# A four-layer mixture kernel: the row mean made once, the second adapter matrix on 128 rows, and stages of the last layers at other steps

## The chip, the cores and the metric

One Trainium2 chip, one core. The metric is device time in microseconds (us): 1599.91 us for the kernel before, median of 3 runs (1598.82 to 1601.06).

## The reference

x has 8 sequences of 256 tokens with 256 features, in float32. Four residual layers follow each other:

```python
x = x + L0(x)   # 2 of 4 experts per sequence (256->1024->256), 3 shared ones, a softmax gate from token 0
x = x + L1(x)   # 8 experts and a shared one, all dense: silu(x @ Wg) * (x @ Wu) @ Wd, weighted per sequence
x = x + L2(x)   # adapter of the sequence's language, then a layer norm
x = x + L3(x)   # y = x @ W[subject].T + b[subject]
```

L2 is the part that the change rewrites most:

```python
h = relu(x @ w1 + b1)                 # 256 -> 64
z = x + h @ w2 + b2                   # 64 -> 256
mean = mean(z); var = mean((z - mean)**2)
L2 = (z - mean) * rsqrt(var + 1e-5) * gamma + beta
```

## The kernel before

The activations lie transposed, features on partitions, in two halves of 128 (`DT` = 2), tokens along the free axis. To keep float32's precision every operand of a product is split into a high and a low part (`fp32r`), and a product is three matmuls: high by high, high by low, low by high (lines 435 to 437). ScalarE copies the high part, VectorE or GpSimd subtracts it for the low part.

L0 and L1 run over blocks of 512 tokens. L1's first eight experts run in 64 stages of `pair_tiles` and `pair_up` (k = 0 to 63), where a scheme of seven products stands for eight. The gate of L0's last block and its mixing into x are not finished when L1 begins: VectorE does them in stages k = 0, 1 and 2. In k = 1 it computes the probabilities (`gate_probs`, lines 1976 to 1978) and mixes the experts' sum ("experts", line 1986) for two sequences behind `gated_tile(k, 2)` and in front of `gated_tile(k, 3)`, and adds x's low part ("lo", line 1988) at the end of the stage. The shared experts follow in k = 2 (line 1990). TensorE's next stage waits for the fourth gated tile.

The ninth (shared) expert of L1, L2 and L3 run together in steps T = 0 to 59 (`last_steps`). A step is one slice of 128 hidden features of one of five jobs: three of 512 tokens, then two of 256 (`LAST_JOBS`). In step T TensorE makes `last_up` of that step (12 products) and `last_down` of step T - 2 (6 products), and then the hooks of the step. From T = 40 on there are hooks alone, but for the last two `last_down`. When job u is complete, VectorE adds it to x (`last_take`, line 2140, in step 8(u+1)), and the unit u of L2 and L3 follows over these tokens, in stages whose steps are written by hand in `WHEN`:

- x2 and xs: x's high and low parts (lines 1359, 2183); for units 1 and 2 the sum of x's two halves (GpSimd, line 1751) and its parts, so that the mean needs two products in place of four.
- up (`l2_up_stage`): x @ w1, 64 output rows. hid: ScalarE makes the relu twice (lines 1383, 1384), VectorE the low part (line 2191), each on 64 rows.
- down (`l2_down_stage`): `mean_part` puts minus the mean of x into both halves of the output in PSUM (lines 810, 814), and three products of w2 with 64 rows each are added to it (lines 834 to 836). w2 and b2 are centred beforehand (lines 2166 to 2175), so that the sum is z less its mean.
- res (line 2202): VectorE adds x and b2. Then the squares (lines 2211, 1760, 1765), gamma (line 1369), the variance (`var_stage`, line 848), eps (line 2218), the power -1/2 (GpSimd, line 1774), a diagonal of it (line 1400), its broadcast by TensorE (`rstd_stage`, line 856), norm and add (lines 2227, 2237), x's new parts, the two halves of L3 (`l3_stage`, lines 872 to 874) and the output with its bias (line 2285).

The last unit (`END`, 4) has a path of its own at the end, in which L3 is applied to parts that are scaled later.

Each engine works its own queue in the order of the program, and within a step in this order: the step's own tile, then the hooks by unit and stage, with those inserted by hand in front or behind. Waits are on semaphores, which count completed instructions of a kind. The banks of `unit_ps` are shared by units 0, 1, 2 and 4: `l2_up_stage` waits for `out_ready`, the output of an earlier unit. SP's queue loads weights; from line 409 on it loads the identity and then, per sequence, w3, w1, w2 and three small vectors (cols: b2, gamma, beta; b1; the bias), into a ring of four buffers `raw`. The eight weights are split in steps 2 to 11 (`center_w2` on VectorE in step b + 2, `late_hi` on ScalarE in b + 3, `late_lo` on GpSimd), and the relu of unit 0 waits for the last of them (line 1377 and after). `b2_stage` (line 785) and `center_b2` (lines 2172 to 2175) centre the bias, in front of all other hooks of step 10.

Of the kernel before, what the change touches and what calls it, by code (L numbers as in the profile page):

```python
# [21 lines left out]
NB = 4  # L22
# [29 lines left out]
STAGES = ["x2", "xs", "up", "hid", "down", "res", "square", "scale", "var", "eps", "diag", "rstd",  # L52
          "norm", "add", "x3", "x3l", "l3a", "outa", "l3b", "outb"]
WHEN = [dict(zip(STAGES, at)) for at in (
# [32 lines left out]
def build(nc, xT_d, sh_d, ex_d, l1_d, types_d, types_row_d, gvec_d, gw1_d, gw2_d, prob_d, sgate_d, w1_d, w2_d, b1_d, cols_d, w3_d, bias_d, ident_d, out_d):  # L87
# [88 lines left out]
    w2 = [place(f"l2_w2_{b}", [A2, 2, D], f32r, over=where_in, skip=2 * K1 * at)  # L176
# [13 lines left out]
    w2s = place("w2_sum", [A2, 1], f32, over="shared_sums", skip=small + 896)  # L190
# [4 lines left out]
    u = place("l2_hidden_r", [A2, 2, BLK], f32r, over="raw", skip=10240)  # L195

    ctx = ExitStack()
    with ctx:
# [40 lines left out]
        small_full = sem("small_full")  # L239
# [10 lines left out]
        hid_relu, sq_first = sem("hid_relu"), sem("sq_first")  # L250
        xs_sum, xs_hi, xs_lo, base_done = sem("x_row_sum"), sem("x_row_hi"), sem("x_row_lo"), sem("base_done")
# [95 lines left out]
        late_small = 3 * B  # L347
# [3 lines left out]
        def _(sp):  # L351
# [58 lines left out]
            for b in range(B):  # L410
                key = ("plain", PLAIN0 + L1_CH * NE1 + b)
# [4 lines left out]
                sp.dma_start(raw[0:A2, s, 640:896], w2_d[langs[b]]).then_inc(raw_full[s], 16)  # L416
                sp.dma_start(cols[:, b], cols_d[langs[b]]).then_inc(small_full, 16)
# [14 lines left out]
        def _(pe):  # L432
# [348 lines left out]
            def b2_stage():  # L781

                pe.wait_ge(small_full, 16 * late_small)
                pe.wait_ge(sum_taken, NB * NJ + 4 * NS)
                pe.matmul(unit_ps[0][:, 1, 0:DT * B], ones[:], cols[:, :, 0:DT], start=True, stop=True).then_inc(b2_sum, 1)

            def l2_up_stage(i):
                b0, nb, t0, c0, n = unit(i)
                pe.wait_ge(w_lo, PLAIN0 + L1_CH * NE1 + b0 + nb)
                if i in (1, 2):  # L790
# [13 lines left out]
            def mean_part(i, m):  # L804
# [3 lines left out]
                if "xs" in WHEN[i]:  # L808
                    for part in range(2):
                        pe.matmul(out, minus_mean[:], xsr[i // 2][:, part, 0:n], start=part == 0, stop=False, skip_group_check=True)  # L810
                    return
# [4 lines left out]

            def l2_down_stage(i):

                b0, nb, t0, c0, n = unit(i)
                if i == 0:  # L820
                    pe.wait_ge(b2_done, 1)
                if "xs" in WHEN[i]:
                    pe.wait_ge(xs_lo, i)
                mean_part(i, 1)
                if i == END:
                    x_part(i, 0)
                pe.wait_ge(hid_relu, i + 1)
                mean_part(i, 0)
                pe.wait_ge(l2_hid, i + 1)
                for b in range(b0, b0 + nb):  # L830
                    c = slice(b % 2 * S, (b % 2 + 1) * S)
                    for m in range(DT):
                        out, k = unit_ps[i][:, m, c], slice(m * P, (m + 1) * P)
                        pe.matmul(out, w2[b][:, 0, k], u[:, 0, c], start=False, stop=False, skip_group_check=True)
                        pe.matmul(out, w2[b][:, 0, k], u[:, 1, c], start=False, stop=False, skip_group_check=True)
                        last = pe.matmul(out, w2[b][:, 1, k], u[:, 0, c], start=False, stop=True, skip_group_check=True)
# [105 lines left out]
            hooks = placed({"up": l2_up_stage, "down": l2_down_stage, "var": var_stage,  # L942
                            "rstd": rstd_stage, "l3a": lambda i: l3_stage(i, 0), "l3b": lambda i: l3_stage(i, 1),
                            "beta": beta_part, "scaled": scaled_part})
            hooks.setdefault(10, []).insert(0, b2_stage)
# [844 lines left out]
        def _(dve):  # L1790
# [278 lines left out]
            def pair_tiles(e, j, s):  # L2069
# [19 lines left out]
                if k == 2:  # L2089
                    mix(0, 0)  # L2090
                    mix(0, 1)
# [276 lines left out]
```

## Time and profile before

| what | value |
|---|---|
| median of 3 runs | 1599.91 us (1598.82 to 1601.06) |
| the profiled execution's own time | 1598.26 us |
| its span | 1596.5 us |
| TensorE busy | 1583.3 us, 99% |
| weight load (beside the matmuls) | 1345.9 us, 84% |
| VectorE busy | 1138.5 us, 71% |
| ScalarE busy | 930.0 us, 58% |
| GpSimd busy | 662.1 us, 41% |
| share of TensorE in the chain that ended last | 93% |
| share of VectorE in that chain | 4% |

The span runs from the first to the last instruction of the profiled execution. In the rows below PE is TensorE, DVE VectorE, ACT ScalarE, POOL GpSimd and SPq the queue of SP. Matmuls are pipelined and their ends are modelled, so that the duration of one is longer than the time that it adds.

### The profile page before, as it was taken

How to read it: one execution, taken by the hardware profiler on the slowest of the kernel's cores; microseconds unless marked ns; L12 is line 12 of the kernel's file. 1: busy time of each engine (PE TensorE's matmuls, PEld its weight loads, DVE VectorE, ACT ScalarE, POOL GpSimd, SP SyncE). 2: the span in 40 equal slices, each digit the busy share in tenths (PEclk: the TensorE clock that was granted, in tenths of full speed). 3: DMA queues.
4: the chain of work that ended last, by engine and by line, in shares of the span. 5: the costliest groups of instructions: out<-in, count | busy, mean ns of one | idle time of the engine just before them, and what ended most of it. 6: DMA issues, size and time to landing. Idle time of an engine off the chain costs nothing.

```text
span 1596.5 us, 22398 instructions
## 1 busy us (share of the span) xinstructions
PE 1583.3 (99%) x7944; PEld 1345.9 (84%) x7944; DVE 1138.5 (71%) x1676; ACT 930.0 (58%) x1680; POOL 662.1 (41%) x576
## 2 busy tenths in 40 slices
PE   9999999999999999999999999999999999999999
PEld 7888888999987888888888888888888888888888
DVE  6755557778889777777776777777777777656556
ACT  5655555665665665565565565565565565554343
POOL 7765544655775431431431431431431431146110
PEclk9999999999999999999999999999999999999999
DMA  4111105455421010010010010010010010021000
GB/s 159 54 54 53 54 27 181 164 185 173 159 84 36 14 41 27 14 40 27 14 40 28 14 40 27 14 40 28 14 41 27 14 40 27 28 58 51 14 14 27
DMA packets 30500, 85.46 MB, mean 54 GB/s; under 512 B 5030, under 2 KB 10022, under 8 KB 30262
## 3 DMA queue, kind: packets, MB, share of 16 engines
q1 hardware_dynamic: 29798, 82.68, 15.1%
q8 instruction: 63, 1.03, 0.3%
q0 software_dynamic: 304, 1.10, 0.2%
q14 instruction: 47, 0.39, 0.1%
q10 hardware_dynamic: 288, 0.26, 0.1%
HBM read 81.93 MB, written 2.10 MB: 53 GB/s over the span
## 4 chain that ended last, share of the span: by engine, by line
PE 93%; DVE 4%; POOL 2%; issue 1%; ACT 1%; DMA 0%; SPq 0%; ACTq 0%; DVEq 0%; POOLq 0%
PE up L666 13%; PE up L668 13%; PE up L667 13%; PE sum L435 12%; PE sum L436 12%; PE sum L437 12%; PE up L435 3%; PE up L436 3%; PE up L437 3%; PE up L443 2%; PE up L444 2%; PE up L445 2%; DVE expert_out L2004 1%; POOL shared_up L1440 1%; DVE hidden L2018 1%
## 5 line engine op out<-in xcount | busy, mean ns | idle before, releaser
L1265 ACT ACTIVATE hidden_hi<-up_tile 128x512 fp32r<-128x512 f32 x256 | 161.2, 630 | 187.7 <-DVE up_tile L2062 163.7
L2057 DVE TENSOR_TENSOR gate_tile<-up,gate_tile 128x512 f32<-128x512 f32 x192 | 129.9, 687 | 141.7 <-PE up L668 141.7
L2067 DVE TENSOR_TENSOR hidden_lo<-up_tile,hidden_hi 128x512 fp32r<-128x512 f32 x256 | 196.7, 788 | 44.7 <-ACT hidden_hi L1265 44.7
L666 PE MATMUL up<-x_sums,gate_up 128*128 128x512 f32 x512 | 199.3, 389 | 0.0
L435 PE MATMUL sum<-hidden_hi,down 128*128 128x512 f32 x512 | 199.3, 389 | 0.0
L437 PE MATMUL sum<-hidden_hi,down 128*128 128x512 f32 x512 | 199.3, 389 | 0.0
L436 PE MATMUL sum<-hidden_lo,down 128*128 128x512 f32 x512 | 199.2, 389 | 0.0
L668 PE MATMUL up<-x_sums,gate_up 128*128 128x512 f32 x512 | 199.2, 389 | 0.0
L667 PE MATMUL up<-x_sums,gate_up 128*128 128x512 f32 x512 | 199.2, 389 | 0.0
L2062 DVE TENSOR_TENSOR up_tile<-up_tile,gate_tile 128x512 f32<-128x512 f32 x192 | 183.8, 983 | 2.3
L1258 ACT ACTIVATE gate_tile<-gate_tile 128x512 f32<-128x512 f32 x192 | 119.7, 632 | 90.4 <-DVE gate_tile L2057 88.3
L1440 POOL TENSOR_TENSOR gate_up<-raw,gate_up 128x384 fp32r<-128x384 f32 x60 | 68.0, 1133 | 204.2 <-ACT gate_up L1209 204.2
L1254 ACT ACTIVATE gate_tile<-up 128x512 f32<-128x512 f32 x192 | 110.6, 594 | 71.2 <-PE up L668 64.8
L666 PE MATMUL up<-x_hi,gate_up 128*128 128x512 f32 x384 | 149.7, 390 | 0.9 <-DVE up_tile L2062 0.9
L667 PE MATMUL up<-x_lo,gate_up 128*128 128x512 f32 x384 | 149.4, 389 | 0.0
L668 PE MATMUL up<-x_hi,gate_up 128*128 128x512 f32 x384 | 149.4, 389 | 0.0
L2057 DVE TENSOR_TENSOR up_tile<-up,up_tile 128x512 f32<-128x512 f32 x192 | 130.0, 687 | 2.6 <-PE up L668 0.7
L1440 POOL TENSOR_TENSOR expert_in<-raw,expert_in 128x512 fp32r<-128x512 f32 x64 | 92.1, 1440 | 89.4 <-ACT expert_in L975 89.3
L1254 ACT ACTIVATE up_tile<-up 128x512 f32<-128x512 f32 x192 | 112.1, 600 | 21.2 <-PE up L668 15.6
L1567 POOL TENSOR_TENSOR weight_sums<-raw 128x256 f32<-128x256 f32 x30 | 28.9, 964 | 204.7 <-PE up L668 204.7
L435 PEld LDWEIGHTS sum<-hidden_hi,down 128*128 128x128 f32 x512 | 96.1, 188 | 20.8 <-DVE hidden_lo L2067 1.2
L666 PEld LDWEIGHTS up<-x_sums,gate_up 128*128 128x128 f32 x512 | 96.1, 188 | 20.3 <-ACT gate_tile L1254 0.4
(323 smaller groups left out, 4031.2 us busy)
## 6 DMA issues: line engine op xcount, KB each, us to landing
raw<-in_experts SPq DMA_DIRECT2D x64, 512.0 KB, 3.2
raw<-in_l SPq DMA_DIRECT2D x51, 512.0 KB, 3.2
raw<-in_shared SPq DMA_DIRECT2D x23, 512.0 KB, 3.3
raw<-in_w SPq DMA_DIRECT2D x8, 256.0 KB, 2.6
x<-in_xT SPq DMA_DIRECT2D x3, 512.0 KB, 9.1
l_stage<-in_l SPq DMA_DIRECT2D x3, 512.0 KB, 4.1
out<-out_stage SPq DMA_DIRECT2D x6, 256.0 KB, 2.6
gate_w<-in_gw POOLq DMA_DIRECT2D x1, 1024.0 KB, 6.1
```

Of the source, the lines that this page charges most:

```text
L435: pe.matmul(out, wh, vh, start=start, stop=False)
L436: pe.matmul(out, wh, vl, start=False, stop=False)
L437: return pe.matmul(out, wl, vh, start=False, stop=stop)
L666: pe.matmul(out, wh, vh, start=first, stop=False, skip_group_check=True)
L667: pe.matmul(out, wh, vl, start=False, stop=False, skip_group_check=True)
L668: return pe.matmul(out, wl, vh, start=False, stop=True, skip_group_check=True)
L1254: A(out, ps, ACT.Copy).then_inc(q_done[m], 1)
L1265: A(hi[:, i], cu[:, i], ACT.Copy).then_inc(hi_done, 1)
L1440: return nc.gpsimd.tensor_tensor(dst, src, hi.bitcast(f32), ALU.subtract)
L2057: V.tensor_tensor(t, ps, t, ALU.add).then_inc(c_done[m], 1)
L2062: V.tensor_tensor(cu[:, i], up, cg[:, RING[i]], ALU.mult).then_inc(gat_done, 1)
L2067: V.tensor_tensor(lo[:, i], cu[:, i], hi[:, i].bitcast(f32), ALU.subtract).then_inc(lo_done, 1)
```

## The change

The mean of x is made once, into the second half of the output (`mean_stage`, at the up stage's step for units 0, 1 and 3, at step 28 for unit 2). VectorE adds it to both halves of x and puts them into y (in `hid_stage`, ahead of the hidden tile's low part), and the residual reads y. w2 is loaded twice, one copy under the other on 128 rows; the high part of the hidden tile stands on rows 0 to 63 and its low part on rows 64 to 127, so that one matmul takes both. The last unit keeps the mean in both halves. Third and fourth unit get other steps, the up stage of units 1 and 2 waits for one output half less, `cols` is loaded ahead of the weights, the bias is centred at the end of step 9's hooks, and the gate's work in stages k = 1 and 2 is ordered anew, with the low part of x added by GpSimd.

```diff
-STAGES = ["x2", "xs", "up", "hid", "down", "res", "square", "scale", "var", "eps", "diag", "rstd",
+STAGES = ["x2", "xs", "up", "mean", "hid", "down", "res", "square", "scale", "var", "eps", "diag", "rstd",
           "norm", "add", "x3", "x3l", "l3a", "outa", "l3b", "outb"]
 WHEN = [dict(zip(STAGES, at)) for at in (
-    (9, 10, 11, 11, 12, 12, 12, 13, 13, 13, 13, 14, 14, 14, 15, 15, 16, 16, 17, 18),
-    (17, 18, 19, 19, 20, 20, 20, 21, 21, 21, 21, 22, 22, 22, 23, 23, 24, 25, 25, 26),
-    (25, 26, 27, 28, 29, 29, 29, 30, 31, 31, 32, 33, 33, 35, 35, 36, 37, 37, 38, 38),
-    (34, 34, 35, 35, 36, 36, 36, 37, 37, 37, 38, 39, 43, 43, 45, 45, 46, 48, 46, 50))]
+    (9, 10, 11, 11, 11, 12, 12, 12, 13, 13, 13, 13, 14, 14, 14, 15, 15, 16, 16, 17, 18),
+    (17, 18, 19, 19, 19, 20, 20, 20, 21, 21, 21, 21, 22, 22, 22, 23, 23, 24, 25, 25, 26),
+    (25, 26, 27, 28, 28, 30, 30, 30, 31, 32, 32, 33, 34, 34, 35, 35, 36, 38, 38, 39, 39),
+    (34, 34, 35, 35, 35, 37, 37, 37, 38, 38, 38, 39, 41, 43, 43, 45, 45, 46, 48, 46, 50))]
...
-    u = place("l2_hidden_r", [A2, 2, BLK], f32r, over="raw", skip=10240)
+    u = place("l2_hidden_r", [2 * A2, BLK], f32r, over="raw", skip=10240)
...
             for b in range(B):
+                sp.dma_start(cols[:, b], cols_d[langs[b]]).then_inc(cols_full, 16)
+            for b in range(B):
...
-                sp.dma_start(raw[0:A2, s, 640:896], w2_d[langs[b]]).then_inc(raw_full[s], 16)
-                sp.dma_start(cols[:, b], cols_d[langs[b]]).then_inc(small_full, 16)
+                sp.dma_start(raw[:, s, 640:896], w2_d[langs[b]]).then_inc(raw_full[s], 16)
...
             def l2_up_stage(i):
...
                 if i in (1, 2):
-                    pe.wait_ge(out_ready, 2 * i)
-                if i == 4:
-                    pe.wait_ge(out_ready, 6)
+                    pe.wait_ge(out_ready, 2 * i - 1)
+                if i == END:
+                    pe.wait_ge(out_ready, 5)
...
+            def mean_stage(i):
+
+                b0, nb, t0, c0, n = unit(i)
+                out = unit_ps[i][:, 1, c0:c0 + n]
                 if i == 0:
                     pe.wait_ge(b2_done, 1)
+                if i in (1, 2):
+                    pe.wait_ge(out_ready, 2 * i)
                 if "xs" in WHEN[i]:
                     pe.wait_ge(xs_lo, i)
-                mean_part(i, 1)
+                    pe.matmul(out, minus_mean[:], xsr[i // 2][:, 0, 0:n], start=True, stop=False)
+                    pe.matmul(out, minus_mean[:], xsr[i // 2][:, 1, 0:n], start=False, stop=True).then_inc(mean_done, 1)
+                    return
+                last = product_of_parts(out, t0, n)
+                last.then_inc(mean_done, 1)
+
+            def product_of_parts(out, t0, n):
+
+                for dt in range(DT):
+                    pe.matmul(out, minus_mean[:], xh[:, dt, t0:t0 + n], start=dt == 0, stop=False)
+                    last = pe.matmul(out, minus_mean[:], xl[:, dt, t0:t0 + n], start=False, stop=dt == DT - 1)
+                return last
+
+            def l2_down_stage(i):
+
+                b0, nb, t0, c0, n = unit(i)
                 if i == END:
+                    pe.wait_ge(out_ready, 6)
+                    mean_part(i, 1)
                     x_part(i, 0)
                 pe.wait_ge(hid_relu, i + 1)
-                mean_part(i, 0)
+                if i == END:
+                    mean_part(i, 0)
+                else:
+                    pe.wait_ge(x_centered, i + 1)
                 pe.wait_ge(l2_hid, i + 1)
...
-                        pe.matmul(out, w2[b][:, 0, k], u[:, 0, c], start=False, stop=False, skip_group_check=True)
-                        pe.matmul(out, w2[b][:, 0, k], u[:, 1, c], start=False, stop=False, skip_group_check=True)
-                        last = pe.matmul(out, w2[b][:, 1, k], u[:, 0, c], start=False, stop=True, skip_group_check=True)
+                        pe.matmul(out, w2[b][:, 0, k], u[:, c], start=i != END, stop=False, skip_group_check=True)
+                        last = pe.matmul(out, w2[b][:, 1, k], u[:, c], start=False, stop=True, skip_group_check=True)
...
-            hooks.setdefault(10, []).insert(0, b2_stage)
+            hooks.setdefault(9, []).insert(0, b2_stage)
...
+                if e == 0:
+                    pool.wait_ge(x_experts, 2)
+                    last_block = slice((NB - 1) * BLK, NB * BLK)
+                    G(x[:, :, last_block], x[:, :, last_block], xl[:, :, last_block].bitcast(f32), ALU.add).then_inc(x_low_added, 1)
                 down_lo(e, 2)
...
             def pair_tiles(e, j, s):
...
                 tile_lo(k, 0)
+                if k == 1:
+                    gate_probs(NB)
+                    mix("experts", 0)
                 if k == 2:
+                    dve.wait_ge(x_low_added, 1)
                     mix(0, 0)
                     mix(0, 1)
...
-                if k == 1:
-                    gate_probs(NB)
-                    mix("experts", 0)
-                    mix("experts", 1)
...
                 tile_lo(k, 1)
                 if k == 1:
-                    mix("lo", 0)
-                    mix("lo", 1)
+                    mix("experts", 1)
...
             def hid_stage(i):
...
+                if i != END:
+                    dve.wait_ge(mean_done, i + 1)
+                    if i:
+                        dve.wait_ge(x3_done, DT * i)
+                    for dt in range(DT):
+                        last = V.tensor_tensor(y[:, dt, c], x[:, dt, t0:t0 + n], unit_ps[i][:, 1, c], ALU.add)
+                    last.then_inc(x_centered, 1)
                 dve.wait_ge(hid_relu, i + 1)
-                V.tensor_tensor(u[:, 1, c], ru[:, c], u[:, 0, c].bitcast(f32), ALU.subtract).then_inc(l2_hid, 1)
+                V.tensor_tensor(u[A2:2 * A2, c], ru[:, c], u[0:A2, c].bitcast(f32), ALU.subtract).then_inc(l2_hid, 1)
...
-            hooks.setdefault(10, []).insert(0, center_b2)
+            hooks.setdefault(9, []).append(center_b2)
...
-        "w2": v["L2_cond_W2"],
+        "w2": np.concatenate([v["L2_cond_W2"], v["L2_cond_W2"]], axis=1),
```

The tiles, copies and sums of w2 go to 128 rows in the same way, and the residual of units 0 to 3 reads y in place of x. GpSimd's new addition stands in front of `down_lo(0, 2)`.

## Rows read from the trace of the kernel before

**Rows 1.** The page, parts 1 (engine, busy us, share, instructions) and 2 (granted clock).

```profile
PE 1583.3 (99%) x7944; PEld 1345.9 (84%) x7944; DVE 1138.5 (71%) x1676; ACT 930.0 (58%) x1680; POOL 662.1 (41%) x576
...
PEclk9999999999999999999999999999999999999999
```

**Rows 2.** TensorE's waits: us in total, times, longest.

```profile
PE sum L435 <- issue: 1.5, 1, 1.5
...
PE up L666 <- DVE up_tile L2062: 0.9, 1, 0.9
...
PE up L814 <- ACT l_hidden_r L1384: 0.8, 1, 0.8
```

**Rows 3.** Timeline of TensorE, unit 0: start, us, engine, line, instruction.

```profile
1463.52 0.28 PE L437 MATMUL sum<-x_hi,l_w 128*64 128x256 f32 x1
1463.63 0.40 PE L435 MATMUL up<-x_hi,last_gate_up 128*128 128x512 f32 x1
1463.86 0.40 PE L436 MATMUL up<-x_lo,last_gate_up 128*128 128x512 f32 x1
...
1469.67 0.39 PE L814 MATMUL sum<-x_lo,minus_mean 128*128 128x512 f32 x1
1469.99 0.38 PE L834 MATMUL sum<-l_hidden_r,l_w 64*128 64x256 f32 x1
1470.22 0.28 PE L835 MATMUL sum<-l_hidden_r,l_w 64*128 64x256 f32 x1
1470.34 0.27 PE L836 MATMUL sum<-l_hidden_r,l_w 64*128 64x256 f32 x1
...
1471.40 0.28 PE L836 MATMUL sum<-l_hidden_r,l_w 64*128 64x256 f32 x1
1471.60 0.50 PE L435 MATMUL up<-x_hi,last_gate_up 128*128 128x512 f32 x1
1471.94 0.40 PE L436 MATMUL up<-x_lo,last_gate_up 128*128 128x512 f32 x1
```

**Rows 4.** Timelines of VectorE and GpSimd, stages k = 1 and 2.

```profile
476.67 1.37 DVE L2057 TENSOR_TENSOR gate_tile<-up,gate_tile 128x512 f32<-128x512 f32 x2 [2.84 <-PE up L668]
...
482.65 1.54 DVE L1986 SCALAR_TENSOR_TENSOR x<-x,gate,x_hi 128x512 f32<-128x512 f32 x2
...
493.83 2.55 POOL L1440 TENSOR_TENSOR down<-raw,down 128x512 fp32r<-128x512 f32 x2 [11.23 <-ACT down L1218]
```

**Rows 5.** Timelines by engine, SP's loads and unit 0.

```profile
1411.11 0.34 SPq L414 DMA_DIRECT2D raw<-in_w  x1
...
1414.13 0.44 SPq L419 DMA_DIRECT2D l_bias<-in_bias  x1
...
1426.83 0.41 DVE L2166 TENSOR_REDUCE w_sum<-raw 64x1 f32<-64x256 f32 x1
...
1464.35 0.22 DVE L2172 TENSOR_SCALAR minus_mean<-ones 128x128 fp32r<-128x128 f32 x1
...
1467.25 0.47 ACT L1383 ACTIVATE l_hidden<-sum,l_b 64x256 f32<-64x256 f32 x1 [0.65 <-POOL l_w L1440]
...
1474.46 1.28 POOL L1765 TENSOR_TENSOR squares<-squares 128x512 f32<-128x512 f32 x1 [0.69 <-DVE squares L2211]
...
1475.84 1.02 PE L848 MATMUL sum<-ones,squares 128*128 128x1 f32 x8
```

**Rows 6.** Timelines by engine: norm of unit 0, then unit 2.

```profile
1482.46 1.28 DVE L2227 TENSOR_TENSOR y<-sum,y 128x512 f32<-128x512 f32 x2
...
1541.21 0.68 DVE L2285 TENSOR_TENSOR out_stage<-sum,l_bias 128x512 f32<-128x512 f32 x1
...
1541.99 0.30 PE L435 MATMUL sum<-x_hi,l_w 128*64 128x256 f32 x1 [1.53 <-issue]
...
1557.95 1.02 POOL L1774 TENSOR_TENSOR rstd<-variance,minus_half 128x4 f32<-128x4 f32 x1 [3.53 <-DVE variance L2218]
...
1559.00 1.28 ACT L1400 ACTIVATE rstd_diag<-ident,rstd 128x128 f32<-128x128 f32 x4 [0.35 <-POOL rstd L1774]
```

More of the change, by code:

```diff
@@ L189, in build @@
     b2s = place("b2_sum", [P, B], f32, over="shared_sums", skip=small + 864)
-    w2s = place("w2_sum", [A2, 1], f32, over="shared_sums", skip=small + 896)
+    w2s = place("w2_sum", [2 * A2, 1], f32, over="shared_sums", skip=small + 896)
     w1r = place("l2_w1", [P, B, 2, DT * A2], f32r, over="gate_w1")
@@ L238, in build @@
         chain = sem("dve_chain")
-        small_full = sem("small_full")
+        small_full, cols_full = sem("small_full"), sem("cols_full")
         x2_done, x2_hi, x2_lo = sem("x2_done"), sem("x2_hi"), sem("x2_lo")
@@ L250, in build @@
         hid_relu, sq_first = sem("hid_relu"), sem("sq_first")
+        x_experts, x_low_added = sem("x_experts"), sem("x_low_added")
+        mean_done, x_centered = sem("mean_done"), sem("x_centered")
         xs_sum, xs_hi, xs_lo, base_done = sem("x_row_sum"), sem("x_row_hi"), sem("x_row_lo"), sem("base_done")
@@ L346, in build @@
         SMALL = 5
-        late_small = 3 * B
+        late_small = 2 * B
         @block.sync
@@ L781, in b2_stage @@
             def b2_stage():
-                pe.wait_ge(small_full, 16 * late_small)
+                pe.wait_ge(cols_full, 16 * B)
                 pe.wait_ge(sum_taken, NB * NJ + 4 * NS)
@@ L807, in mean_part @@
                 out = unit_ps[i][:, m, c0:c0 + n]
[L808 to L811, printed above, removed]
                 for dt in range(DT):
@@ L941, in _ @@
                         pair_up(e, j, s)
-            hooks = placed({"up": l2_up_stage, "down": l2_down_stage, "var": var_stage,
+            hooks = placed({"up": l2_up_stage, "mean": mean_stage, "down": l2_down_stage, "var": var_stage,
                             "rstd": rstd_stage, "l3a": lambda i: l3_stage(i, 0), "l3b": lambda i: l3_stage(i, 1),
                             "beta": beta_part, "scaled": scaled_part})
-            hooks.setdefault(10, []).insert(0, b2_stage)
+            hooks.setdefault(9, []).insert(0, b2_stage)
             def last_step(T, tok, N):
@@ L1383, in hid_hi_stage @@
                     A(ru[:, c], unit_ps[i][0:A2, 0, c], ACT.Relu, bias=b1[:, b:b + 1])
-                    last = A(u[:, 0, c], unit_ps[i][0:A2, 0, c], ACT.Relu, bias=b1[:, b:b + 1])
+                    last = A(u[0:A2, c], unit_ps[i][0:A2, 0, c], ACT.Relu, bias=b1[:, b:b + 1])
                 last.then_inc(hid_relu, 1)
@@ L1991, in mix @@
                                                  ALU.mult, ALU.add)
-                if part != NSH - 1:
+                if part == "experts" and tb == NB:
+                    ins.then_inc(x_experts, 1)
+                elif part != NSH - 1:
                     linked(ins)
@@ L2196, in res_stage @@
                 dve.wait_ge(l2_down, i + 1)
-                if i:
-                    dve.wait_ge(x3_done, DT * min(i, 3))
+                if i == END:
+                    dve.wait_ge(x3_done, DT * 3)
+                else:
+                    dve.wait_ge(x_centered, i + 1)
                 for dt in range(DT):
```

23 lines of the change are left out of this document (13 added, 10 removed).

## The prediction

> **What bounds the kernel now.** Read part 1 of the page first: TensorE is busy for 99% of the span, the next engine for 71% [rows 1], and the granted clock is at its full level in every slice. So a change pays only by what it takes off TensorE's stream or out of its pauses. Then the list of TensorE's waits [rows 2]: they are few. Three of them lie where the change works: 0.9 us behind VectorE's up_tile in the gate's stretch, 1.5 us put down as "issue" and 0.8 us behind the hidden tile. Then the timeline for the pace: the durations (0.39 us) overlap and are no price; what an instruction costs is the distance to the next start, 0.23 us for 512 columns (1463.63, 1463.86) and 0.12 for 256 (1470.22, 1470.34) [rows 3]. One late step is 18 products: 4.08 us with 512 columns (18 x 0.2267), 2.16 with 256.
>
> **The gate (steps of the first expert).** VectorE makes the gate's shares and the mix of both halves (1.54 us) in front of the last gated tile, for which TensorE waits [rows 4]. After the change shares and half a mix stand in front of the tiles of 476.67, where VectorE sat idle for 2.84 us [rows 4]; they need about 1.7 us (0.9 for three small instructions, 0.77 for half of the pair). The other half comes after the last gated tile. The pause goes: 0.9 us and some 0.2 for the restart, 1.1 us. The low part's addition moves to GpSimd, one pass of 1,024 columns; the nearest row is two passes of 512 in 2.55 us [rows 4], so some 2.5. GpSimd was idle for 11.23 us there, until 493.83 [rows 4], and VectorE needs the result only for the next step's mix, some 5 us after. I take nothing; without that cover it would be up to 3 us.
>
> **What leaves TensorE in the five units.** The mean was made in both output halves: units 0 and 3 lose four products, units 1 and 2 two each, 8 x 0.227 + 4 x 0.12 = 2.3 us. The second matrix's three products become two: 16 x 0.12 = 1.9 us. Around these 64-row products lie gaps: 0.32 and 0.23 at the first (1469.67, 1469.99, 1470.22) and, from 1471.40, 0.20 and 0.34 in leaving [rows 3], against 0.23, 0.12, 0.12 and 0.23 by the pace: some 0.4 us a unit, 2.0 in all. Below is nothing, if the gaps belong to the waits that stand at the same places; above is the 0.4. I take 0.4, since a product behind the 64-column stage starts 0.11 after it though it is behind a wait as well (1463.52, 1463.63 [rows 3]). The Trainium skill's page "TensorEngine Tiling (Array Packing)", Key Properties, says that a change of tiling mode drains TensorE, and counts 128x64 as a mode too. By that rule the gain of 2.0 stands, but the 64-column stage should show gaps, and the row shows none; without any drain the sum would be 2.0 smaller.
>
> Were nothing late elsewhere, that would be 6.2 us, with the gate's 1.1 and the waits of the units (1.6, 1.0 and 0.2) 10.1. But the mean's result now goes through VectorE: two additions (1.28 us by [rows 6], the same operands' kinds) stand ahead of the hidden tile's low part, and TensorE waits for both.
>
> **Unit 0.** Centring the bias moves ahead of step 10's tile on VectorE. It is three small instructions, the first 0.22 us [rows 5]; with the waits between them I take 0.5. It was behind the tile; now ScalarE's copy of the tile, the eighth weight's high part and GpSimd's low part come 0.5 later, and the hidden tile, begun at 1467.25, waited for just that (0.65 us behind POOL l_w [rows 5]). Its four copies then end at about 1469.3 and the low part (0.69) near 1470.2. TensorE gets there sooner: 1463.63 + four means 0.93 + a step 4.08 = 1468.6. It pauses 1.6 us, and eight products end at 1471.2, against 1471.60 before [rows 3]: 0.4 gained. VectorE, later by 0.4, makes the squares later too; they ended at 1475.74 (1474.46 + 1.28) and the variance started at 1475.84 [rows 5], so they already decided. They end near 1476.2 while TensorE is there at 1475.3. Net **0.4 lost**. The doubled matrix (128 rows where 64 stood) costs each engine nothing by rows, as durations go by columns; bound above: every one doubled, 0.4 us at each of three engines on this path, 1.5 in all. On SP eight small loads now stand ahead of the first weights; each takes 0.6 us of the queue (1411.11 to 1414.13 is five issues), 5 us together. VectorE's first use of what they delay is at 1426.83 [rows 5], 15.7 after, and each later batch is shorter by 0.6. Nothing; without cover up to 5.
>
> The low part of the hidden tile is written to rows 64 to 127, from rows 0 to 63. The Trainium skill's "VectorE: DVE Perf Modes", "Two Vector instructions with no wait between them", holds such an instruction until the earlier ones have ended, against the overlap of 0.08 us that rows show. By it unit 0 would come another 0.1 to 0.2 later. No row here has such a write; my sum leaves that to the range.
>
> **Unit 1.** Off TensorE go 0.46 (mean), 0.48 (four products) and 0.4 (gaps), 1.3; its hidden tile has a whole step of cover, so no pause there. But VectorE gets to the residual only 0.8 earlier, and the variance hangs on the squares as in unit 0. **0.8 gained**.
>
> **Unit 2.** The 1.5 us "issue" are really the output's second half: VectorE works at it until 1541.89 (1541.21 + 0.68), TensorE starts at 1541.99 [rows 6]. The up stage no longer waits for it, the mean does, one step later: 1.6 gained, plus 0.46, 0.48 and 0.4, is 2.9. Then comes a new wait. The eps now stands on VectorE at step 32, behind the sum taken from step 33's product. From the end of that product 1.3 us for sum and eps, 1.02 for the power and 1.28 for the diagonal [rows 6], with hand-overs 4.0; TensorE needs only one step of 2.16 until it wants it at step 34: a pause of 1.8, where it paused 0.4 to 0.5 before. With the rest **2.0 remain**, bounds 1.0 and 2.9.
>
> **Unit 3.** The 0.8 us pause behind the hidden tile goes, with its restart 1.0; four means, two products and the gaps are 0.48, 0.24 and 0.4: 2.1. Given back are about 0.7 (the low part of x is late, VectorE being busy with unit 2's norm) and 0.9 (the variance, again behind the squares); later pauses of about 0.5 in front of the last unit shrink. **1.0 gained**. **Last unit**: two products 0.24 and the gaps 0.4, **0.6**, for its end is a chain through TensorE.
>
> **The sum** is 1.1 - 0.4 + 0.8 + 2.0 + 1.0 + 0.6 = 5.1 us. The profiled execution took 1598.26 us (span 1596.5 and 1.8 around it), so 1593.2 for it; it lies 1.65 below the median 1599.91, and I forecast the median: **1594.8 us**. About 0.2%, 3.2 us, is what a measurement of this kernel can tell from no change.
>
> **Rivals.**
> *The whole stream is gained* (0.12): VectorE keeps up everywhere, 10.1 us, 1589.8. For it: VectorE is busy only 71%. Against it: in unit 0 the squares and the hidden tile set the time already.
> *Less is gained* (0.20): the 64-row gaps are waits and remain (2.0), and VectorE's hand-overs cost 0.2 more in each of four units: 5.1 - 2.8 = 2.3, 1597.6. For it: at both places with gaps stands a wait.
> *Slower* (0.06): the new pauses at steps 12, 13, 34 and 38 make TensorE's clock fall. Place: from step 34 on, the 1.8 us pause. About 19 us of products follow; at the lower level, 1.2 instead of 2.4 GHz, they take twice that. If half of them run so, it costs 9.5: 1594.8 + 9.5 = 1604. It decides from a third of them on (5.1 us). Against it: the longest pause now, 1.53 us before 1541.99 [rows 6], lies in a slice at the full level, as all do [rows 1].
> *My forecast* (0.62): its own range is 1592 to 1597.
>
> The range, 1590.0 to 1598.6, takes in the forecast's bounds, most of the second case and nearly all of the first, and leaves out the slow one. Faster: 0.55 of the forecast, 0.12 and 0.09, 0.76. Within: 0.18. Slower: 0.06.
>
> **What would show it.** Right: no TensorE wait behind up_tile near 485 and no "issue" near 1540; no 0.2 us gaps around the second matrix; a wait of one to two us behind the hidden tile of unit 0, one before each variance, one behind rstd_diag at step 34. The forecast is wrong if TensorE has none of the new waits (then 1590), if the gaps stay (1597), or if the time changed somewhere outside of 470 to 500 and of the last 140 us.

## The result, and the profile of the kernel after

The changed kernel takes 1593.8 us (median; 1592.89 to 1595.73), the kernel before 1599.45 us in the same sessions: a ratio of 0.9965 with a 95% interval of 0.9952 to 0.9978. That is 5.65 us less, and faster by more than 0.2%. The forecast was 1594.8 us, range 1590.0 to 1598.6.

The page of the kernel after, parts 1 and 2 (its profiled execution took 1593.19 us):

```profile
span 1591.4 us, 22366 instructions
...
PE 1577.5 (99%) x7916; PEld 1342.9 (84%) x7916; DVE 1144.1 (72%) x1682; ACT 929.8 (58%) x1680; POOL 664.8 (42%) x577
...
PEclk9999999999999999999999999999999999999999
```

TensorE has 28 instructions fewer than before [rows 1], twelve means and sixteen products of the second matrix, and is 5.8 us less busy. It still bounds the kernel, at 99%. TensorE's waits in the kernel after (us in total, times, longest):

```profile
PE sum L858 <- DVE l_hidden_r L2226: 1.5, 1, 1.5
PE sum L879 <- ACT rstd_diag L1423: 1.3, 1, 1.3
...
PE sum L871 <- POOL squares L1792: 1.0, 2, 0.7
...
PE up L871 <- DVE squares L2249: 0.4, 1, 0.4
```

All three rows of [rows 2] are gone: "issue", up_tile and ScalarE's hidden tile. In their place stand these four rows, 4.2 us together, at places that the prediction named. One sign of its list is missing: nothing waits in front of unit 2's variance. TensorE's timeline shows where each stands: unit 0's second matrix, unit 0's variance, unit 2's rstd, unit 3's variance.

```profile
1468.04 0.39 PE L440 MATMUL sum<-hidden_hi,last_down 128*128 128x512 f32 x1
1469.88 0.36 PE L858 MATMUL sum<-l_hidden_r,l_w 128*128 128x256 f32 x1 [1.46 <-DVE l_hidden_r L2226]
1470.08 0.28 PE L859 MATMUL sum<-l_hidden_r,l_w 128*128 128x256 f32 x1
...
1475.85 1.05 PE L871 MATMUL sum<-ones,squares 128*128 128x1 f32 x8 [0.67 <-POOL squares L1792]
...
1559.87 1.13 PE L879 MATMUL sum<-rstd_diag,ones 128*128 128x512 f32 x2 [1.29 <-ACT rstd_diag L1423]
...
1573.32 1.02 PE L871 MATMUL up<-ones,squares 128*128 128x1 f32 x8 [0.43 <-DVE squares L2249]
```

What a single profiled execution says of a few tenths depends on where one measures. The distance between two products of TensorE that both kernels have is what to compare; in the late steps it repeats from run to run to within 0.1 us, where whole times scatter by 2. "First matrix" is the first 64-column product of a unit, rstd is L856 before and L879 after:

| stretch on TensorE | before | after | difference | forecast |
|---|---|---|---|---|
| gate: last product with expert_out (456.70, 457.48) to the first with gate_up after the pairs of k = 1 to 3 (511.05, 510.74) | 54.35 | 53.26 | -1.09 | -1.1 |
| first late product to unit 0's first matrix | 50.56 | 50.57 | 0 | 0 |
| to unit 0's rstd | 18.67 | 19.12 | +0.45 | +0.4 |
| to unit 1's rstd | 41.58 | 40.84 | -0.74 | -0.8 |
| to unit 3's first matrix | 43.09 | 41.31 | -1.78 | -2.0 |
| to the last unit's first matrix | 20.00 | 18.05 | -1.95 | -1.0 |
| to the end of the last product | 8.12 | 7.48 | -0.64 | -0.6 |

The sum is -5.75, against -5.65 by the medians. Between the gate's stretch and the late steps the kernels differ by 0.1 us in 900. Ahead of the gate's stretch the profiled execution of the kernel after is 0.78 us the longer one (457.48 against 456.70), though the program is the same there; the last section shows a fall of the clock in that part. The forecast's 0.7 us for the low part of x in front of unit 3 stands in its unit 3, but in the table that wait ends the row above, "to unit 3's first matrix". From unit 0's first matrix to the end it is 131.46 us before and 126.80 after; below this is called **the tail**, and the experiments are read by it.

The gate's stretch on VectorE and GpSimd, after:

```profile
474.55 0.15 DVE L2003 TENSOR_REDUCE gate_sum<-gate_exp 128x2 f32<-128x8 f32 x1
...
475.85 1.47 DVE L2013 SCALAR_TENSOR_TENSOR x<-x,gate,x_hi 128x512 f32<-128x512 f32 x1
...
485.13 2.78 POOL L1731 TENSOR_TENSOR x<-x,x_lo 128x1024 f32<-128x1024 f32 x1 [1.29 <-DVE x L2013]
493.52 2.56 POOL L1463 TENSOR_TENSOR down<-raw,down 128x512 fp32r<-128x512 f32 x2 [5.60 <-ACT down L1241]
```

Shares and half a mix now run from 474.55 on, in the time in which VectorE was idle [rows 4]; they take 2.8 us and not 1.7, and still fit. The three small instructions take 1.3 us, as they did before (1.28, from 481.37 to 482.65), where the prediction had 0.9; the half mix takes 1.47 beside GpSimd's weights, where it had 0.77. GpSimd's pass takes 2.78 us (2.5 forecast), and GpSimd is idle behind it for another 5.60. Beside that pass one low part of VectorE, of 512 columns, took 2.29 us in place of 0.68 (at 486.18); TensorE waited for nothing there.

### The profile page after: what moved, and what is told of

Read it like the earlier page. It is cut to its first block, busy times and chain, and to the rows that moved or that the text cites. A ratio compares the mean times of both kernels' runs of the same rounds, so it can differ in the third digit from the quotient of the medians.

```text
span 1591.4 us, 22366 instructions
## 1 busy us (share of the span) xinstructions
PE 1577.5 (99%) x7916; PEld 1342.9 (84%) x7916; DVE 1144.1 (72%) x1682; ACT 929.8 (58%) x1680; POOL 664.8 (42%) x577
## 4 chain that ended last, share of the span: by engine, by line
PE 92%; DVE 5%; POOL 2%; ACT 1%; issue 1%; DMA 0%; SPq 0%; ACTq 0%; POOLq 0%; DVEq 0%
PE up L669 13%; PE up L670 13%; PE up L671 13%; PE sum L438 12%; PE sum L439 12%; PE sum L440 12%; PE up L438 3%; PE up L439 3%; PE up L440 3%; PE up L446 2%; PE up L447 2%; PE up L448 2%; DVE expert_out L2033 1%; POOL shared_up L1463 1%; DVE hidden L2047 1%
```

## The experiments

Each edit is to the changed kernel, unless it says otherwise. The kernel before measured 1599.1 to 1599.7 us beside them.

### The gate's order of before

```
 k == 1, in front of the tiles:   - gate_probs(NB); mix("experts", 0)
 in front of the last gated tile: + gate_probs(NB); mix("experts", 0); mix("experts", 1)
 behind it:  - mix("experts", 1)   + mix("lo", 0); mix("lo", 1)
 GpSimd:     - x = x + x_lo
```

> The changed kernel with the gate's order of before: shares and both halves of the experts' mix in front of the last gated tile of step 2, the low part added by VectorE. Theory (the gate is worth 1.1 us): the time is 1.1 us above the changed kernel's 1593.8, so 1594.9, and TensorE shows again a wait of 0.9 us behind up_tile; the stretch from the start of the gate's steps to the first product of the next step group takes 57.0 us as before, not 56.0. Rival (the 1.1 us less in that stretch is not the order of VectorE's work but the scatter of one profiled execution): 1593.8, and no wait behind up_tile.

Measured: 1594.96 us, ratio 0.9971 (0.9960 to 0.9982). The gate's stretch took 54.36 us, against 53.26 after and 54.35 before, and the pause was back. The expectation's 57.0 and 56.0 are the same stretch begun some 2.7 us earlier; they differ by 1.0. TensorE's timeline of this kernel:

```profile
487.43 0.50 PE L669 MATMUL up<-x_hi,gate_up 128*128 128x512 f32 x1 [0.85 <-DVE up_tile L2085]
```

The tail stayed at 126.72. So the gate's part is worth 1.1 us, and by itself.

### 64 rows in place of 128

```
- pe.matmul(out, w2[b][:, 0, k], u[:, c], ...)
+ pe.matmul(out, w2[b][0:A2, 0, k], u[0:A2, c], ...)      (the same for part 1)
```

> The changed kernel with its two products of the second matrix reading rows 0 to 63 alone of weight and hidden tile (same count, same waits, same columns; it leaves out the product of the hidden tile's low part). Theory of the forecast (passing from 128 rows to 64 and back costs TensorE 0.2 us each way): gaps of 0.3 where the first of these products starts and of 0.2 more behind the last, in each of five units; 2.0 us if all of it stands on the path, so 1595.8, and at least 1594.6 if the variance waits of three units absorb theirs. Rival (the gaps of before were the waits that stood at the same places): products 0.12 us apart as with 128 rows, 1593.8.

Measured: 1594.3 us, ratio 0.9970 (0.9958 to 0.9982); the tail is 127.46, 0.66 more. TensorE's timeline of this kernel in unit 1, where TensorE is held up by nothing:

```profile
1511.22 0.39 PE L440 MATMUL sum<-hidden_hi,last_down 128*128 128x512 f32 x1
1511.54 0.38 PE L858 MATMUL sum<-l_hidden_r,l_w 64*128 64x256 f32 x1
1511.76 0.28 PE L859 MATMUL sum<-l_hidden_r,l_w 64*128 64x256 f32 x1
1511.88 0.28 PE L858 MATMUL sum<-l_hidden_r,l_w 64*128 64x256 f32 x1
...
1512.47 0.28 PE L859 MATMUL sum<-l_hidden_r,l_w 64*128 64x256 f32 x1
1512.67 0.50 PE L438 MATMUL up<-x_hi,last_gate_up 128*128 128x512 f32 x1
```

With no pause at either end the gaps are back: 0.32 and 0.22 on entering, 0.20 in leaving, where the pace gives 0.23, 0.12 and 0.12. With the one behind (0.34 for 0.23) that is 0.38 us a unit. The same place of the kernel with 128 rows, with the same semaphore waits in the program, has 0.12 from one product to the next and 0.23 behind the 512 columns. So the gaps belong to the rows and not to the waits: the rival of hand-overs falls. But the tail grew by 0.66 and not by 1.9: in units 0, 1 and 3 the wait in front of the variance shrank by the same amount (0.67 to 0.47, 0.33 and 0.43 to none listed), and only unit 2 (0.3) and the last unit (0.4) pay.

### The doubled matrix alone, on the kernel before

```
- w2[b] [A2, 2, D], u [A2, 2, BLK];  three products: hi x hi, hi x lo, lo x hi
+ w2[b] [2 * A2, 2, D], u [2 * A2, BLK];  two products of 128 rows
```

> The kernel before with the doubled second matrix alone: two products of 128 rows in place of three of 64, the low part of the hidden tile written to rows 64 to 127; steps, means, bias and gate as before. Theory: 1.9 us of products and up to 2.0 us of gaps go, in units 0 to 3 a part of it is given back in front of the variance (0.1 to 0.4 a unit, since the residual starts earlier by the same and VectorE is free for it), so 3.0 to 3.9 us below the kernel before (1599.45), 1595.5 to 1596.5; the doubled work of three engines costs nothing. Rival one (gaps are waits): 1.9 us, 1597.6. Rival two (the write to the other rows, or the doubled weight work, costs on the path): under 1.5 us gained.

Measured: 1597.11 us, ratio 0.9982 (0.9973 to 0.9991); tail 128.80, 2.66 less than before. That is under both ends of the theory (3.0 to 3.9) and above rival one. By the table's stretches it gains 0.17 in unit 0 and 0.60 to 0.64 in each of the others. The products and gaps of units 1 and 2 add up to 0.86 (0.48 + 0.38), and 0.2 of it is given back; unit 3 and the last unit keep their 0.62 (0.24 + 0.38) whole. The weight work of 128 rows delayed nothing: the hidden tile's first copy starts 5.0 us behind unit 0's first product in both kernels. The write to rows 64 to 127 took 0.69 us, as did the one to the other half, but VectorE's next instruction started 0.72 us behind it and not 0.61.

### The relaxed wait of the first matrix alone, on the kernel before

```
 up:   - pe.wait_ge(out_ready, 2 * i)      + pe.wait_ge(out_ready, 2 * i - 1)
 down: + pe.wait_ge(out_ready, 2 * i)      (in front of the means)
```

> The kernel before with one change: the first products of units 1 and 2 wait for the first half of the output before them, and the mean for the second half. Theory (the 1.5 us put down as issue at unit 2 is the wait for the output's second half): that pause goes and nothing takes its place, since the mean stands 0.23 us x 12 and more behind; 1.5 us less, 1597.9, and no issue in TensorE's waits. Rival (it is a pause of TensorE's own queue, or the mean now waits in its place): no gain, or the pause stands at the mean, 1599.45.

Measured: 1598.11 us, ratio 0.9993 (0.9984 to 1.0002), which is 1.6 below the 1599.73 beside it but can't be told from no change by its interval. The tail can tell: 129.73, 1.73 less, all of it in front of unit 2, and TensorE's list has no "issue" any more. The pause of [rows 6] was the wait for the output's second half.

### Both of these parts, on the kernel before

The last two diffs together.

> The kernel before with the doubled second matrix and the relaxed wait of the first matrix's products together: means still made in both output halves, steps and gate as before. Theory (the two parts add up, and the mean made once with its moved steps is worth only the rest): stretch 131.5 - 2.7 - 1.7 = 127.1 against 126.8 of the changed kernel, so the mean made once gave 0.3 us net of the 2.3 us of products that it takes off; 1595.0. Rival (the mean made once gave its 2.3): the two parts don't add up, stretch 129, 1597.

Measured: 1595.39 us, ratio 0.9975 (0.9965 to 0.9985); tail 127.10, as expected to the tenth. So the two parts add up, and the rest of the change, the mean made once with the steps and the bias moved for it, takes the tail from 127.10 to 126.80 only. By the table's stretches this rest loses 0.60 us to unit 0's rstd and 0.59 between unit 1's rstd and unit 3's first matrix, and gains 0.09 in unit 1 and 1.35 in unit 3, where the pause behind the hidden tile and those in front of the last unit go. So of the 2.3 us of products that it removes, 2.0 were given back, net of the pauses that it ends.

### The steps of before for units 2 and 3

```
 unit 2: - down 30, var 32, diag 33, rstd 34     + down 29, var 31, diag 32, rstd 33
 unit 3: - down 37, var 38, diag 39, rstd 41     + down 36, var 37, diag 38, rstd 39
 (and the stages beside them, such as eps, scale and unit 2's L3, one step earlier)
```

> The changed kernel with the steps of before for units 2 and 3 (second matrix at 29 and 36, variance at 31 and 37, rstd at 33 and 39), the mean at 28 and 35. Theory (with the additions ahead of it the hidden tile needs a second step of cover): TensorE waits some 0.3 us behind unit 2's hidden tile and 1.5 us behind unit 3's, against 0.9 us saved at rstd_diag: 0.9 us more, 1594.7. Rival (the moved steps were what gave the gain): the 1.5 to 2 us of units 2 and 3 go, 1597. Rival two (they did nothing): 1593.8.

Measured: 1594.05 us, ratio 0.9970 (0.9959 to 0.9980); tail 127.86, 1.06 more. TensorE's waits in this kernel:

```profile
PE sum L858 <- DVE l_hidden_r L2226: 2.0, 2, 1.5
PE up L858 <- DVE l_hidden_r L2226: 1.3, 1, 1.3
...
PE sum L879 <- ACT rstd_diag L1423: 0.4, 1, 0.4
```

0.5 at unit 2's hidden tile (2.0 less unit 0's 1.5), 1.3 at unit 3's, 0.4 at the diagonal (from 1.3, so 0.9 saved): the theory's 0.3, 1.5 and 0.9. The moved steps are what the additions on VectorE need, and worth 1.1 us with them.

### The bias centred two steps earlier

```
- hooks.setdefault(9, []).insert(0, b2_stage)     + hooks.setdefault(7, []).insert(0, b2_stage)
- hooks.setdefault(9, []).append(center_b2)       + hooks.setdefault(7, []).append(center_b2)
```

> The changed kernel with the centring of the bias two steps earlier, on TensorE and on VectorE. Theory (what the change moved ahead of step 10's tile, 0.42 us, stands on the chain to unit 0's hidden tile): TensorE's wait behind that tile falls from 1.46 to 1.0 us, 0.4 us less in all, 1593.4. Rival (ScalarE or GpSimd has slack there): the wait stays at 1.4 to 1.5.

Measured: 1592.67 us, ratio 0.9961 (0.9946 to 0.9976); tail 126.54, 0.26 less; the wait fell from 1.46 to 1.27. The direction is the theory's, the size half. TensorE's own product for the bias costs 0.24 us with its gaps (1453.22 to 1453.91 in the kernel after, where the pace gives 0.45). It stood right behind the sum that VectorE takes into x, and now stands two steps ahead of it; so that sum, step 9's tile and the low part of x came 0.24 us later, measured from unit 0's first matrix, and of 0.42 us 0.18 were left.

### The eighth weight at step 9

```
 VectorE: center_w2(7)  - at the end of step 9     + at the head of step 9's extra work
 ScalarE: late_hi(7)    - at the head of step 10   + at the end of step 9's extra work
```

> The changed kernel with the eighth weight made ready earlier: centred at the head of step 9's extra work on VectorE (idle there for 0.86 us), its high part at the end of ScalarE's step 9 instead of step 10. Theory (unit 0's hidden tile is late because ScalarE waits for GpSimd's low part of this weight, and nothing else): the wait of 1.46 us behind the hidden tile goes, unit 0 ends 1.0 to 1.5 us earlier, 1592.3 to 1592.8. Rival one (VectorE's two additions are what is late): the wait stays above 1.0, since they start behind step 10's low part at 1467.75 in any case. Rival two (the variance waits in its place): TensorE gets there earlier and waits 1.5 to 2 us behind the squares instead of 0.7; gain under 0.5.

Measured: 1592.62 us, ratio 0.9960 (0.9946 to 0.9973); tail 126.28, 0.52 less. The wait behind the hidden tile halved, to 0.70, which is neither the theory (gone) nor rival one (above 1.0), and the variance did not take over: it stayed at 0.67. VectorE's timeline of this kernel, and then GpSimd's, show what took its place:

```profile
1459.48 2.52 DVE L2212 TENSOR_TENSOR x_lo<-x,x_hi 128x512 fp32r<-128x512 f32 x2
1461.92 0.76 DVE L2201 TENSOR_SCALAR minus_mean<-ones 128x128 fp32r<-128x128 f32 x1
...
1462.79 1.08 DVE L2204 SCALAR_TENSOR_TENSOR b_centered<-b_sum,l_cols 128x16 f32<-128x16 f32 x1
```

```profile
1459.00 5.95 POOL L1464 TENSOR_TENSOR l_w<-raw,l_w 128x512 fp32r<-128x512 f32 x6 [3.83 <-ACT l_w L1376]
```

GpSimd now subtracts two weights without a break, and beside it the bias's small instructions take 0.76 and 1.08 us on VectorE, where the kernel after has 0.21 and 0.17. TensorE's mean waits for the bias, and its first two products were late by 0.3 us together, so that some 0.5 of the 0.76 us remained.

### Unit 2's rstd at step 35

```
- unit 2: rstd 34, norm 34        + rstd 35, norm 35
```

> The changed kernel with unit 2's rstd product and norm at step 35 instead of 34. Theory (the wait of 1.3 us behind rstd_diag is the new wait of the changed steps, and one step of 2.16 us more covers it): it goes, 1.3 us less, 1592.5. Rival (the norm and the addition now meet unit 3's centred x and hidden tile on VectorE): no wait at rstd_diag, but one of about 1 us behind unit 3's hidden tile or its x_lo; no gain.

Measured: 1593.39 us, ratio 0.9965 (0.9952 to 0.9979), so no gain that can be told; the tail of the profiled execution is 128.24, 1.44 more. The wait behind rstd_diag is gone and its place is taken by three: 0.34 at unit 3's x_lo, 0.52 at its hidden tile, and 0.88 in place of 0.43 at its variance. By these 1.74 in place of 1.72 the tail would be as long as after. The other 1.4 us are in the windows of this kernel (from and to, length, busy time of PE, PEld, DVE, ACT, POOL, granted clock, DMA share, GB/s):

```profile
1571.00:1574.00 3.00, 2.12 (x20) 1.95 (x18) 2.12 (x6) 1.02 (x4) 0.61 (x1) 1.00 0.00 0
1574.00:1577.00 3.00, 3.00 (x20) 3.00 (x20) 1.09 (x3) 1.14 (x4) 0.70 (x1) 0.66 0.27 89
1577.00:1580.00 3.00, 3.00 (x22) 3.00 (x22) 1.17 (x3) 1.13 (x4) 0.00 (x0) 0.77 0.01 4
1580.00:1583.00 3.00, 3.00 (x26) 2.95 (x25) 2.17 (x6) 0.81 (x2) 0.00 (x0) 1.00 0.26 87
```

The granted clock was at its lower level, 1.2 GHz, from 1574.9 to 1578.3. In that time TensorE's 256-column products stood 0.213 us apart, against 0.12 at the full level of 2.4 GHz:

```profile
1574.77 0.28 PE L438 MATMUL up<-x_hi,last_gate_up 128*128 128x256 f32 x1
1574.89 0.33 PE L439 MATMUL up<-x_lo,last_gate_up 128*128 128x256 f32 x1
...
1577.57 0.41 PE L440 MATMUL sum<-hidden_hi,last_down 128*128 128x256 f32 x1
1577.79 0.41 PE L895 MATMUL sum<-l_w,x_hi 128*128 128x256 f32 x1
...
1578.42 0.28 PE L895 MATMUL sum<-l_w,x_hi 128*128 128x256 f32 x1
```

What TensorE did before was two pauses within 6 us, 0.68 at 1568.26 and 1.04 at 1573.45 with their restarts, and then eight one-column products. The kernel after has the same one-column products and one pause of 0.60 there, and the kernel with the old steps one of 1.48 at 1568.87; both keep their clock. So the prediction's third rival, a fall of the clock in the late steps, does occur, though not at its place and with 1.4 us and not 9.5; that the pauses bring it on is argued from this one profile. Not each execution seems to have it: of the five, two have a mean clock of 0.998 (this one with 1594.8 us, and 1595.38) and three 0.999 (1592.22 to 1593.39).

### Unit 2's eps and diagonal one step earlier

```
- unit 2: eps 32, diag 33         + eps 31, diag 32
```

> The changed kernel with unit 2's eps in VectorE's step 31 and its diagonal in ScalarE's step 32 instead of 32 and 33; TensorE's order is not touched. Theory (the eps is late because it stands behind step 32's tile and the sum taken from step 31's product on VectorE: the variance ends at 1554.2, the eps comes at 1557.3): eps, power and diagonal end some 2 us earlier, the wait of 1.3 us behind rstd_diag goes, and the stretch from the first product of unit 0's first matrix to the end falls from 126.8 to 125.4; 1592.4. Rival (VectorE, now held at the variance, brings the next tiles late): TensorE waits behind up_tile or hidden_lo in steps 32 to 34 instead, and nothing is gained. Whether the clock falls after unit 3's pauses, as it did when the rstd product was moved to step 35, is to be seen in the stretch.

Measured: 1591.54 us, ratio 0.9953 (0.9939 to 0.9966); tail 125.30, 1.50 less. VectorE's timeline, first of the kernel after and then of this one:

```profile
1556.47 0.88 DVE L2168 SCALAR_TENSOR_TENSOR x<-sum,l_coef,x 128x256 f32<-128x256 f32 x2
1557.26 0.15 DVE L2256 TENSOR_SCALAR variance<-sum 128x4 f32<-128x4 f32 x1
```

```profile
1555.18 0.16 DVE L2256 TENSOR_SCALAR variance<-sum 128x4 f32<-128x4 f32 x1 [0.86 <-PE sum L871]
1556.07 0.42 DVE L2179 TENSOR_TENSOR up_tile<-up,gate_tile 128x256 f32<-128x256 f32 x1 [0.73 <-ACT gate_tile L1359]
```

VectorE waits 0.86 us at the eps now, and then 0.73 for its next tile: it held nothing up. The wait behind rstd_diag is gone, none came in its place, and the clock did not fall in the tail. So the eps was late only by its place in VectorE's order.

### The three moves together

The diffs of the bias, of the eighth weight and of the eps together.

> The changed kernel with three of the moves together: bias centred two steps earlier, eighth weight at step 9, unit 2's eps and diagonal at 31 and 32. Theory: in unit 0 the small instructions of the bias no longer run beside GpSimd (0.76 and 1.08 us there, 0.2 each without), so the 0.7 us left of the wait behind the hidden tile go with the 0.3 in front of the mean: stretch 126.8 - 1.5 (hidden tile) - 1.4 (rstd_diag) = 123.9, and 1590.9 us. Rival (each saving is taken back by the variance, whose squares start no earlier): the wait before unit 0's variance grows from 0.7 to over 1.5, and the stretch stays above 125.

Measured: 1591.01 us (1590.76 without the execution named next), ratio 0.9949 (0.9935 to 0.9962). The profiled execution took 9048.49 us: TensorE's 512-column products lasted some 1,693 ns each against 389, at a granted clock given as 1.0, while VectorE and ScalarE were busy for 1034 and 947 us, about as always. Why stays open; the same kernel ran once more.

> The same kernel as c2_early once more, for a profile: the one taken there was of an execution in which every product of TensorE took four times as long, and its rows can't be used. Theory: 1590.9 us, stretch 123.9, no wait behind the hidden tile of unit 0 and none behind rstd_diag. Rival: the wait before unit 0's variance over 1.5 us, stretch above 125.

Measured: 1591.24 us, ratio 0.9949 (0.9935 to 0.9962); tail 123.62 (123.9 expected), 3.18 less than the kernel after. TensorE's timeline at unit 0's second matrix:

```profile
1471.42 0.40 PE L440 MATMUL sum<-hidden_hi,last_down 128*128 128x512 f32 x1
1471.65 0.28 PE L858 MATMUL sum<-l_hidden_r,l_w 128*128 128x256 f32 x1
```

Both large waits are gone, and the variance did not take them over: in the late steps TensorE's list keeps 1.0 and 0.4 us behind the squares, as after. To unit 0's rstd the two moves together give 1.74 us (17.38 for 19.12), where the bias alone gave 0.23 and the eighth weight alone 0.49: with the bias out of step 9, TensorE's mean starts on its pace (0.12 us behind the product ahead of it), where with the eighth weight alone it came 0.3 us late. This version beats both kernels: 2.6 us below the changed one by the medians, 8 us below the one before.

## Why the prediction came out right

**The gate** (1.1 us): right, by its stretch (1.09) and by the first experiment (1.1). What it moves was mis-sized, 1.7 us for 2.8, but lay under 2.84 us of idle time, so it cost nothing by a margin of 0.1. The cover on GpSimd held: 2.78 us, with 5.60 of idle time left.

**The 64-row gaps** (0.4 a unit, taken over nothing): right in cause and size. With 64 rows and no wait beside them they cost 0.38 us a unit. The Trainium skill's page "TensorEngine Tiling (Array Packing)", Key Properties, has every change of tiling mode drain TensorE: for 128 rows to 64 and back the trace agrees, with 0.2 us each way. It counts 128x64 as a mode too, and there the trace does not agree. TensorE's timeline of the kernel after, around unit 2's first matrix, has 0.12 us in entering and 0.11 in leaving, so the measurement decides:

```profile
1539.49 0.28 PE L440 MATMUL sum<-hidden_hi,last_down 128*128 128x256 f32 x1
1539.61 0.28 PE L438 MATMUL sum<-x_hi,l_w 128*64 128x256 f32 x1
...
1540.87 0.28 PE L440 MATMUL sum<-x_hi,l_w 128*64 128x256 f32 x1
1540.98 0.28 PE L438 MATMUL up<-x_hi,last_gate_up 128*128 128x256 f32 x1
```

**The doubled matrix at no cost**: right for the weights (the bound above it, 1.5 us, is 1.2 by its own terms, three engines at 0.4). For the write to the other rows, which the sum left to the range, the rows show the hold of 0.1 us. VectorE's timeline of the kernel before, and then of the kernel after:

```profile
1468.84 0.69 DVE L2191 TENSOR_TENSOR l_hidden_r<-l_hidden,l_hidden_r 64x512 fp32r<-64x512 f32 x1 [1.07 <-ACT l_hidden_r L1384]
1469.45 0.68 DVE L2151 TENSOR_TENSOR up_tile<-up,gate_tile 128x512 f32<-128x512 f32 x1
```

```profile
1467.75 1.27 DVE L2223 TENSOR_TENSOR y<-x,sum 128x512 f32<-128x512 f32 x2
1469.05 0.69 DVE L2226 TENSOR_TENSOR l_hidden_r<-l_hidden,l_hidden_r 64x512 fp32r<-64x512 f32 x1
1469.77 0.69 DVE L2179 TENSOR_TENSOR up_tile<-up,gate_tile 128x512 f32<-128x512 f32 x1
```

Before, the next instruction starts 0.08 us ahead of the write's end. After, the write starts 0.03 us behind the end of the additions, and the next instruction 0.03 us behind the end of the write. That is 0.11 us twice on VectorE's path to unit 0's squares, inside the size that the prediction named.

**Unit 0** (0.4 lost): right, +0.45, with a pause of 1.6 at the hidden tile (1.46 of it listed as wait, the rest restart) for 1.6 and of 0.83 at the variance (0.67 listed) for 0.9. The chain named was the right one: moving the bias or the eighth weight shortens that wait, and both together end it.

**Unit 1** (0.8 gained): 0.74, with 0.33 us in front of the variance.

**Unit 2** (2.0 gained): 1.78, or 1.93 without the low part of x, which the prediction has in unit 3. The "issue" was the output's second half, worth 1.73 for 1.6. The pause at the diagonal is 1.45 with its restart for 1.8, and the reason given for it, the eps behind step 32's tile and the sum, is shown by moving the eps alone. That the term met the measured value is in part luck: 2.9 less a pause grown from 0.4 or 0.5 to 1.8 is some 1.5 and not 2.0, and no row stands for the difference. The pause grew by 1.05 (0.40 before) in place of 1.35, and the output's half gave 0.1 more, which makes up for it.

**Unit 3** (1.0 gained): this term was mis-sized. Its stretch gained 1.95, and with the low part of x, which ends the stretch before it, the term is 1.80. The step that failed is what the prediction gives back, "about 0.7" for the late low part of x and 0.9 for the variance. Measured are 0.15 for the low part (the first matrix starts 0.27 us behind the start of the product ahead of it, at 1563.13, where the pace gives 0.12) and 0.60 for the variance with its restart, 0.75 in place of 1.6. Pauses of 0.55 us in front of the last unit went too, where 0.5 was forecast. Why the low part of x was late by so little was not tried.

**The sum** was 5.1 and is 5.75 by the stretches: 0.8 too little in unit 3, and 0.1 or less in each other term. **The rivals**: the whole stream (10.1 us) was not reached by this kernel, with 4.2 us of new waits; with three stages moved 8.9 of it were by the stretches (7.9 by the medians), so VectorE can keep up nearly everywhere if the order lets it. Less gained by hand-overs fell with the 64-row run. The clock's fall did not come in the tail of the changed kernel, and did come, for 3.4 us, in a neighbour of it with two pauses close together.

## What to carry to other kernels

Work taken off the bounding engine counts only as far as the chain that feeds it gets shorter too: here 2.3 us of products gave 0.3 of the tail, and with three stages moved the tail is 3.5 us below that of the kernel with two means. (Whether those moves would help that kernel too was not tried.) So cost the new waits unit by unit and look, at each, for the stage that stands behind foreign work in its engine's order; an eps of 0.15 us, taken out from behind a tile and a sum, gave 1.5 us. Compare distances between two products that both kernels have, for they resolve tenths where whole times scatter by two microseconds.

## What the runs showed of the chip beyond that

**A fall of the clock that comes and goes.** At the end of the gate's small products TensorE's granted clock falls for some microseconds in 11 of 13 usable profiles, that of the kernel after among them, and not in that of the kernel before. The windows of the kernel after, and then of the kernel before:

```profile
313.00:316.00 3.00, 3.00 (x18) 3.00 (x17) 2.03 (x8) 1.11 (x3) 0.00 (x0) 0.55 0.00 0
316.00:319.00 3.00, 3.00 (x24) 3.00 (x24) 2.34 (x5) 1.81 (x4) 1.30 (x1) 0.88 0.54 180
```

```profile
313.00:316.00 3.00, 3.00 (x27) 3.00 (x26) 2.25 (x10) 1.51 (x5) 0.00 (x0) 1.00 0.00 0
316.00:319.00 3.00, 3.00 (x27) 3.00 (x26) 2.86 (x7) 2.20 (x5) 1.29 (x1) 1.00 0.53 180
```

Ahead of it TensorE ran 24 products of 8 columns and 8 of 2, from 308.8 to 312.3; the kernel before ran the same ones, from 309.0 to 312.5. The two profiles without the fall there (the kernel before, and the one with two means, which has a lower stretch at 6 to 12 us instead) lie 1.65 and 1.28 us below the medians; those with it lie from 0.8 below to 2.2 above. The mean clocks of the 24 executions of the kernel before beside the first experiments go the same way: 1597.82 us on average at 1.0 (four), 1599.56 at 0.999 (14), 1600.89 at 0.998 (five). In the nine of the kernel with two means there is no such order (1595.05 at 0.999, 1595.04 at 0.998). So this is a likely source of the scatter of two microseconds, and not shown to be all of it. The 40 slices of the page, 40 us each, don't show it: the digit stays at 9.

**VectorE beside GpSimd.** With GpSimd subtracting weights at the same time, VectorE's small bias instructions took 0.76 and 1.08 us in place of 0.21 and 0.17, its two low parts of x 2.52 in place of the 1.28 that they take with GpSimd idle, and a half of the gate's mix 1.47 in place of 0.74. A few columns are no protection: it was the instruction of 16 columns that took 1.08.
